# The fourth weighing of an attention unit writes to another PSUM bank, from unit 8 on

## What is computed

```python
def _gqa(q, k, v):
    scale = 1.0 / np.sqrt(q.shape[-1])
    scores = jnp.einsum('bsghd,btgd->bghst', q, k) * scale
    p = jax.nn.softmax(scores, axis=-1)
    return jnp.einsum('bghst,btgd->bsghd', p, v)
...
core = _gqa(q, k, v).reshape(b, s, nh * d)
...
xout = _gqa(qx, kx, vx).reshape(b, s, nh * d)
cat = jnp.concatenate([core, xout], axis=-1)
catq = _div_clamp_fp8(cat, proj_smooth)
return jnp.einsum('bsi,oi->bso', catq, wproj) * (proj_in_scale * proj_w_scale)
```

## Time and profile before

| | us |
|---|---|
| median of 3 executions | 736.61 (736.22 to 738.57) |
| the profiled execution, its time | 738.12 |
| its span, first to last instruction | 736.3 |
| PE busy | 639.0 (87%) |
| DVE busy | 553.8 (75%) |
| ACT busy | 420.9 (57%) |
| POOL busy | 266.2 (36%) |
| mean granted TensorE clock | 0.975 |

### The profile page before, as it was taken

How to read it: one execution, slowest core, us unless ns; L and a number is a source line. 1 busy time by engine, 2 the same in 40 slices (tenths; PEclk the granted TensorE clock), 3 DMA queues, 4 the chain that set the end, 5 groups by cost and what they waited for, 6 DMA issues and landing times.

```text
span 736.3 us, 12912 instructions
## 1 busy us (share of the span) xinstructions
PE 639.0 (87%) x4273; PEld 507.6 (69%) x4311; DVE 553.8 (75%) x1349; ACT 420.9 (57%) x1370; POOL 266.2 (36%) x358
## 2 busy tenths in 40 slices
PE   5356989988889999999899999998999999986936
PEld 3245767776677877877687778776887887765724
DVE  7995779978576758877977678778664657688587
ACT  4246757766577645656666456567654666652431
POOL 3104543433232543433245433333341333434251
PEclk9997999999899999999999999999999999998978
DMA  8166474566462203334233122232342322220001
GB/s 265 58 210 225 153 257 185 187 203 205 144 224 101 96 12 104 113 101 125 102 114 83 75 101 103 101 106 101 100 109 86 101 103 106 108 73 1 0 1 57
DMA packets 33211, 86.47 MB, mean 117 GB/s; under 512 B 2910, under 2 KB 28154, under 8 KB 28282
## 3 DMA queue, kind: packets, MB, share of 16 engines
q1 hardware_dynamic: 32960, 85.63, 35.5%
q10 hardware_dynamic: 186, 0.02, 0.0%
HBM read 71.99 MB, written 13.65 MB: 116 GB/s over the span
## 4 chain that ended last, share of the span: by engine, by line
PE 59%; DVE 26%; DMA 5%; ACT 4%; issue 4%; POOL 1%; DVEq 0%; SPq 0%; ACTq 0%
PE bank L538 14%; PE bank L659 14%; PE bank L642 10%; PE bank L546 7%; DVE Cb L1648 3%; DMA WQ<-wq_split 3%; PE bank L611 3%; PE bank L683 3%; PE bank L643 2%; PE bank L673 2%; DMA wq_split<-stage 2%; PE bank L628 1%; DVE stage L1594 1%; DVE nm L1633 1%; DVE ro L1646 1%
## 5 line engine op out<-in xcount | busy, mean ns | idle before, releaser
L659 PEld LDWEIGHTS bank<-V,Pt 128*128 128x128 f32 x1024 | 128.0, 193 | 55.9 <-DVE Cb L1648 44.1
L659 PE MATMUL bank<-V,Pt 128*128 128x129 f32 x1024 | 142.1, 282 | 20.8 <-DVE Cb L1648 18.7
L987 ACT ACTIVATE square<-bank 128x128 bf16<-128x128 f32 x384 | 101.2, 276 | 98.5 <-PE bank L538 58.2
L538 PE MATMUL bank<-WQ,xq 128*128 128x256 f32 (+1 forms) x1024 | 136.8, 286 | 7.7 <-DMA WQ<-wq_split 3.3
L538 PEld LDWEIGHTS bank<-WQ,xq 128*128 128x128 f32 x1024 | 127.5, 193 | 21.3 <-DVE nm L1633 10.2
L642 PE MATMUL bank<-QT,KTt 128*128 128x512 f32 x256 | 132.7, 600 | 2.0 <-POOL diag L1239 2.0
L1633 DVE TENSOR_REDUCE nm<-bank 128x2 f32<-128x512 f32 x128 | 82.1, 683 | 48.2 <-PE bank L628 48.1
L970 ACT ACTIVATE Pt<-bank 128x512 f32<-128x512 f32 x128 | 76.7, 599 | 72.8 <-remote 46.2
L1225 POOL TENSOR_TENSOR rs<-ve,mhalf 128x6 f32<-128x6 f32 x64 | 95.1, 1487 | 5.3
L1239 POOL TENSOR_TENSOR diag<-identb,nm 128x512 bf16<-128x512 bf16 x64 | 67.0, 1047 | 73.4 <-DVE nm L1633 73.3
L1648 DVE SCALAR_TENSOR_TENSOR Cb<-bank,ro,ism 128x128 bf16<-128x128 f32 x256 | 78.0, 347 | 4.5
(11 more groups left out here) (222 smaller groups left out, 1007.1 us busy)
## 6 DMA issues: line engine op xcount, KB each, us to landing
WQ<-wq_split SPq DMA_DIRECT2D x30, 1536.0 KB, 9.6
wq_split<-stage SPq DMA_DIRECT2D x6, 1536.0 KB, 6.2
ism<-smooth_inverse SPq DMA_DIRECT2D x32, 256.0 KB, 6.4
wst<-in_L_xattn_wproj SPq DMA_DIRECT2D x16, 256.0 KB, 5.1
wq_split<-WQ SPq DMA_DIRECT2D x2, 1536.0 KB, 5.6
wst<-in_L_xattn_wq SPq DMA_DIRECT2D x8, 256.0 KB, 4.9
wst<-in_L_xattn_wqx SPq DMA_DIRECT2D x8, 256.0 KB, 5.4
wst<-in_L_xattn_w_kv_x SPq DMA_DIRECT2D x16, 128.0 KB, 4.3
```

Source lines behind the costliest of these rows:

```text
L538: last = nc.tensor.matmul(o[:, o0:o0 + n], xq[b % 2][:, p, k, ts], WQ[u % 2][:, part, k, w0:w0 + n], start=m == 0, stop=m == 2 * KT - 1)
L659: last = nc.tensor.matmul(o[:, h * (P + 2):h * (P + 2) + P + 1], Pt[:, x, k, h * S + t * P:h * S + (t + 1) * P], V[u % 2][:, x, k, 0:P + 1 ...
L987: last = A(square[:, t, h], head(t, h), ACT.Square, accum_out=ss[:, t, h:h + 1])
```

## The change

`weigh_bank` now also takes x. From unit 8 (G is 8) to unit 30 the weighing with x = 1 and t = 1, the fourth, goes to XB; the other three stay in OB. The fourth waits for XB to be free and for `o_evac` at n-1 in place of n. The first weighing of the units after 8 also waits for n-1 only. After a fourth weighing, XB counts as read when `o_evac` reaches n+1. Unit 31 keeps its banks.

```diff
-        def weigh_bank(u, t):
-
-            return QB[3] if u == UNITS - 1 and t else OB
+        def weigh_bank(u, x, t):
+
+            if u == UNITS - 1:
+                return QB[3] if t else OB
+            return XB if u >= G and x and t else OB
...
                 n = 4 * u + 2 * x + t
-                o = weigh_bank(u, t)
-                if o is OB:
-                    free(OB)
+                o = weigh_bank(u, x, t)
+                if o is OB or o is XB:
+                    free(o)
                 if n:
-                    pe.wait_ge(s["o_evac"], n if u < UNITS - 1 else n - 1)
+                    early = u == UNITS - 1 or o is XB or (u > G and x == 0 and t == 0)
+                    pe.wait_ge(s["o_evac"], n - 1 if early else n)
+                if o is XB:
+                    reader[XB.name] = (s["o_evac"], n + 1)
                 pe.wait_ge(s["exp_done"], 4 * u + 2 * x + 2)
-                if o is not OB:
+                if o is QB[3]:
                     pe.wait_ge(s["max_ready"], 4 * UNITS)
...
                 dve.wait_ge(s["pv_done"], n + 1)
-                o = weigh_bank(u, t)
+                o = weigh_bank(u, x, t)
```

## The result

| | before | changed |
|---|---|---|
| median, us | 737.59 (4 executions) | 728.18 (4 executions, 726.99 to 728.67) |
| ratio | 1 | 0.9863, 95% interval 0.9823 to 0.9902 |
| span of the profiled execution, us | 736.3 | 726.9 |
| first weighing of unit 8 to first weighing of unit 31, us | 423.34 | 413.91 |

The kernel is 9.4 us faster, inside the range that was forecast (726.5 to 733.0) and 2.2 us beyond the forecast gain of 7.2. By the times alone the gain lies between 7 and 13 us, so they don't show by themselves that the forecast fell short; the traces do. The last line of the table is the best measure for what follows. It is the distance between two rows of the timeline (the starts of two matmul groups of the weighings) and holds the 23 touched units and nothing else.

A forecast was written before the change was run, and what follows sets the result against it. PE's wait for DVE's read of the weighing's bank (line 1648) was taken to stand on the path. 6.20 + 0.91 + 0.05 = 7.16, say 7.2 us, off the median 736.61 gives 729.4; range 726.5 to 733.0 (8 in 10).

The forecast's parts named there:

- The place of the wait and what it hid: PE's fourth weighing waits for DVE line 1648 to read the bank; 0.41 us idle shows in 16 of 23.
- What one removed wait gives: In unit 26 project(u+2,0) can start 1.35 us after the guard, not 1.93: 0.58 us to gain.
- a weighing holds it 0.91 us: Time a weighing holds PE in unit 26 (587.25 to 588.16); with 0.44 us after the guard it made 1.35.
- The 13 free units: Units 8, 9, 13, 15 to 17, 21, 23 to 27, 29: next waits move with PE, gain lasts; 6.20 us.
- The paced units: Units 10, 11, 12, 18, 19, 20, 28: DVE sets when project(u+2,1) starts; 0.13 us each, 0.91 us.
- the late guard: In units 8, 9, 12, 17, 20, 25 the guard came late and hid part of the wait; 0.28 to gain.
- Units 13 and 21: Earlier `rs` in unit 12 shortens the next unit's wait a little; shrinking waits here counted only in the upper bound, 8.6.
- Units 14, 22 and 30: project(u+2,0) is left out there and the gain becomes longer waits; 0 for 14 and 22, 0.05 us for 30.
- The waits added: Two wait instructions a unit on PE, costed at nothing; 1.9 us if each of 46 took a tenth of 0.41.
- The full gain: Rival: every unit gains in full, 11.4 us, so 725.2; 8 in 100.
- The wait that takes its place: Rival: another wait holds the fourth weighing at once, little is left, about 736 (735 to 737); 11 in 100.
- The collision of DVE and POOL: Rival: slower by the shared port in the ten units, 0.95 us per collision, 748 at two in each; 5 in 100.

The follow-up runs named there:

- The run with the bank alone: Changed kernel, but the fourth weighings, on XB, wait for the read of the third as before, and so do the first weighings; 737.29 us, ratio to before 0.9999.
- with them alone: The change made only in units 8, 9, 13, 15 to 17, 21, 23 to 27 and 29; 730.44 us, ratio to before 0.9908.
- the run of the paced units alone: The change made only in units 10 to 12, 14, 18 to 20, 22, 28 and 30; 735.89 us, ratio to before 0.9977.
- the run with four more: Changed kernel with four more PE waits, on values long reached, in front of each fourth weighing; 728.80 us, ratio to before 0.9887.
- the kernel with the ends moved: Changed kernel with stats3 and, from unit 8 on, the ends of steps 3, 4 and 5 behind the maxima on DVE; 736.18 us, ratio to before 0.9984.
- stats3 moved: Changed kernel with stats3 in unit 28 moved behind the maxima of unit 29 on DVE; 728.09 us, ratio to before 0.988.
- guard first: Changed kernel; in unit 30 guard(31,1) goes ahead of two of three transpose groups, its maxima ahead of normalise3; 726.77 us, ratio to before 0.9845.
- the kernel with both edits: Changed kernel with four of six stats3 statistics put into unit 27, and unit 30's guard ahead of two transpose groups; 726.56 us, ratio to before 0.9841.

## Why the prediction was right, and where it was short

**The place of the wait and what it hid: right.** The fourth weighing has no idle time in front of it in any of the 23 units, and unit 26 lasts 16.05 us (forecast 16.1). The run with the bank alone shows that the wait, and not the bank, was the cost.

**What one removed wait gives: 0.58 forecast, 0.67 measured.** The step that was mis-sized is "a weighing holds it 0.91 us". That distance was read in the earlier trace rows from a weighing that had just waited. Such a group takes 1.16 us there and 1.06 us when it follows without a stop, and the projection follows it 0.82 us after its start (579.20 to 580.02). Here a wait on PE thus costs its idle time, the lost overlap of 0.16 us and about 0.1 us more in the group behind it. Over 13 units that is 1.2 of the 2.3 us that the forecast fell short.

**The 13 free units: right**, 6.20 forecast, 7.46 measured with them alone.

**The paced units: right in kind.** Units 12, 20 and 28 gained 0.17, 0.16 and 0.15, forecast 0.13. The mechanism is the one given: in unit 26 the reciprocal starts 0.09 us before the maxima's end (580.83 against 580.92), was 0.06 after it. Units 10, 18, 11 and 19 gained 0.22 and 0.31. I had called them paced by DVE because DVE came to the maxima with no idle time. But PE had not waited for them. Unit 11 before, then changed (PE and DVE):

```profile
310.36 1.02 PE L642 MATMUL bank<-QT,KTt 128*128 128x512 f32 x2
...
310.44 1.28 DVE L1633 TENSOR_REDUCE nm<-bank 128x2 f32<-128x512 f32 x2
...
311.24 2.15 PE L538 MATMUL bank<-WQ,xq 128*128 128x256 f32 x16
...
313.23 1.08 PE L546 MATMUL bank<-WC,vT 128*128 128x256 f32 x4
```

```profile
308.49 1.02 PE L644 MATMUL bank<-QT,KTt 128*128 128x512 f32 x2
...
309.10 1.28 DVE L1638 TENSOR_REDUCE nm<-bank 128x2 f32<-128x512 f32 x2
...
309.35 0.38 PE L645 MATMUL bank<-diag,onesb 128*128 128x512 bf16 x1
...
309.84 2.06 PE L540 MATMUL bank<-WQ,xq 128*128 128x256 f32 x16
...
311.73 1.08 PE L548 MATMUL bank<-WC,vT 128*128 128x256 f32 x4
```

The distance from the scores to the last row, the context part of the projection, tells how late PE is (the matmul of line 643 has no record in the first block, so the gap in front of the projection doesn't). It is 2.87 us in unit 26, where nothing holds PE (583.25 to 586.12), and 2.87 or 2.88 in all 13 free units of both kernels. In unit 11 it is 2.87 before and 3.24 changed: PE and DVE had been level, and PE could move forward until DVE held it. What the distance grew and what the unit gained add up to what one removed wait gives: 0.37 + 0.31 here, 0.46 + 0.22 in unit 10 (2.88 to 3.34), 0.52 + 0.15 in unit 28 (3.14 to 3.66) and, with the late guard, 0.22 + 0.17 in unit 12 (3.06 to 3.28). So the step "comes to the maxima with no idle time, so project(u+2,1) starts when DVE says" was right for units 12, 20 and 28 and wrong for 10, 11, 18 and 19, which put them at 0.13 too. That is 0.6 us of the shortfall.

**Units 13 and 21: missed.** The text named the effect (`rs` earlier in unit 12 shortens a wait of the next unit) and left it out of the sum. It gave 0.23 us each, shown by the run of the paced units alone; 0.5 us in all. DVE's wait for `rs` at the end of unit 12, before and in that run:

```profile
330.84 0.69 DVE L1613 TENSOR_TENSOR Qn<-bank,rs 128x512 f32<-128x512 f32 x1 [0.41 <-POOL rs L1225]
```

```profile
328.80 0.69 DVE L1618 TENSOR_TENSOR Qn<-bank,rs 128x512 f32<-128x512 f32 x1 [0.18 <-POOL rs L1230]
```

The wait is 0.23 us shorter. DVE's read of the first weighing of unit 13 then ends early enough for the second one, whose group takes 1.06 us in place of 1.16.

**Units 14, 22 and 30: right**, 0.01 us each. In unit 30 the idle time of PE before the transposes of h3 rose from 1.19 to 1.86 us, the whole 0.67.

**The waits added: about right.** Nothing forecast, 0.01 us a unit by the run with the bank alone and at most 0.04 by the run with four more; the bound of 1.9 us is twice the larger of the two.

**The rivals.** The full gain fell with the run of the paced units. The wait that takes its place fell with the trace. The collision of DVE and POOL did not come: the five quantise steps kept their lengths in the ten units (0.42, 0.43, 0.43, 0.69 and 0.69 us in both kernels). That a loss on DVE can be as large shows in the kernel with the ends moved, where its order alone cost 8 us.

## What to carry to other kernels

If an in-order engine waits for the read of the one bank that it writes, a second bank is worth its idle time and what the restart costs (0.41 and 0.26 us here), but only in those stretches where what comes next also moves with that engine. List, place by place, what is late next, and ask not only whether that engine was busy but whether anybody waited for it; two engines that are level still leave some room. And before moving work on the engine that sets the pace, look at what idle time it filled where it stood: a piece that fits into a gap is best cut to the size of the gaps.

## What was not expected of the hardware

In three profiles (four more waits, stats3 moved, guard first) the granted clock of TensorE fell in unit 30, right behind its idle time before the transposes of the last layer, 1.8 to 2.9 us. Kernel with stats3 moved, 645 to 650 us, then the changed kernel, 647 to 652 us (us, busy time and instructions of PE, PEld, DVE, ACT, POOL, granted clock, DMA share, GB/s):

```profile
645.00:650.00 5.00, 4.34 (x16) 2.59 (x17) 3.51 (x8) 1.19 (x2) 1.06 (x2) 0.66 0.00 0
```

```profile
647.00:652.00 5.00, 4.14 (x19) 2.36 (x20) 3.96 (x9) 2.34 (x4) 1.55 (x11) 1.00 0.01 2
```

A mean of 0.66 over five microseconds is a mix of the two levels, 1.2 and 2.4 GHz. Unit 30 lasted 16.98 us there and 15.86 in the changed kernel; at the fourth weighing of unit 31 0.5 us of this is left (21.07 against 20.59), since the path is DVE's. The changed kernel has the same idle time of 1.86 us and kept the clock in its profile; the kernel before, with 1.19 us, kept it too, and the kernel with both edits kept it behind 2.89 us. In all, the three profiles with 1.2 us of idle time there kept the clock, and three of the eight with 1.8 us or more lost it. What decides stays open, and whether the timed executions have the dip can't be seen. Taking waits away upstream made the idle time at this place longer; that the risk of a dip came with it fits these counts, but eleven profiles don't show it.
